# Fourteen tiles fetched by SyncE instead of seven, GpSimd waiting by itself, and 16-bit control tables in a four-layer graph network

## What is computed

```python
h = jnp.maximum(_layernorm(x, axis=-1), 0.0)
x = x + _L0_gnn_ref(...)   # mean of the source rows, times a weight
x = x + _L1_gnn_ref(...)   # sum of h[src] * edge_weight, two products, leaky relu, row norm
x = x + _L2_gnn_ref(...)   # sum of (h W)[src] * network(edge_attr_128), then a small network
x = x + _L3_gnn_ref(...)   # four-head attention: softmax over the edges of each dst
return x
```

## Time and profile before

| | |
|---|---|
| median of three runs | 4121.83 us |
| span of the profiled execution, from its first to its last instruction | 4118.2 us |
| GpSimd busy | 2981.3 us, 72% |
| VectorE, TensorE, ScalarE busy | 2593.0, 2408.9, 1816.6 us |
| gathers by GpSimd (L756) | 3100, mean 945 ns |
| row transfers by SyncE (L805) | 3584 |

### The profile page before, as it was taken

How to read it: one execution, slowest core, us unless ns; L and a number is a source line. 1 busy time by engine, 2 the same in 40 slices (tenths; PEclk the granted TensorE clock), 3 DMA queues, 4 the chain that set the end, 5 groups by cost and what they waited for, 6 DMA issues and landing times. The chain is left out here.

```text
span 4118.2 us, 65293 instructions
## 1 busy us (share of the span) xinstructions
PE 2408.9 (58%) x13340; PEld 2021.0 (49%) x13340; DVE 2593.0 (63%) x7266; ACT 1816.6 (44%) x4202; POOL 2981.3 (72%) x3172
## 2 busy tenths in 40 slices
PE   3666666655566666656544444444566666666667
PEld 2555555554454555546434334443554555454556
DVE  5444444443566666667644444444669999999997
ACT  3444444422243444432211111111457887788886
POOL 4777777776777777777677777777757777777763
PEclk8787777777677787877765666656779999999899
DMA  7444444432344443432333333333466222222221
GB/s 148 125 116 126 116 126 116 126 83 69 94 116 125 116 124 115 126 106 67 100 110 105 110 105 105 110 105 109 115 117 124 58 57 58 57 57 57 57 53 32
DMA packets 242878, 405.96 MB, mean 99 GB/s; under 512 B 68322, under 2 KB 141691, under 8 KB 242492
## 3 DMA queue, kind: packets, MB, share of 16 engines
q0 software_dynamic: 99456, 206.27, 20.8%
q10 hardware_dynamic: 69920, 120.96, 10.4%
q1 hardware_dynamic: 73116, 74.56, 6.2%
HBM read 331.90 MB, written 67.79 MB: 97 GB/s over the span
## 5 line engine op out<-in xcount | busy, mean ns | idle before, releaser
L756 POOL DMA_INDIRECT t_work<-d_T,t_tabG x3100 | 2928.1, 945 | 1038.5 <-issue 848.1
L1657 PE MATMUL ps<-t_work,t_acc 128*128 x2592 | 463.0, 340 | 439.7 <-POOLq L723 396.5
L1657 PEld LDWEIGHTS ps<-t_work,t_acc 128*128 128x128 f32 x2592 | 414.9, 245 | 516.9 <-issue 516.6
L1730 DVE TENSOR_TENSOR t_acc<-t_acc,ps 128x128 f32 (+1 forms) x732 | 210.3, 287 | 513.6 <-PE ps L594 209.5
L1832 ACT COPY ps<-t_acc 128x512 f32 x244 | 140.6, 588 | 779.1 <-POOLq L723 777.1
L1719 DVE TENSOR_TENSOR t_hT<-t_work,ps 128x512 f32<-128x512 f32 x244 | 167.2, 685 | 503.0 <-ACT ps L1832 502.9
L1657 PE MATMUL ps<-t_hT,t_acc 128*128 128x128 f32 x1296 | 264.0, 388 | 272.2 <-DVE t_acc L1730 263.4
L1657 PEld LDWEIGHTS ps<-t_hT,t_acc 128*128 128x128 f32 x1296 | 249.1, 295 | 288.9 <-DVE t_hT L1719 285.0
L1657 PE MATMUL ps<-t_work 128*128 x1312 | 239.9, 347 | 249.7 <-POOLq L723 220.2
L627 ACT ACTIVATE t_acc<-ps,t_bcol 128x1024 f32<-128x1024 f32 x98 | 109.1, 1113 | 612.4 <-DVE ps L640 590.5
L2145 PE MATMUL ps<-t_work,t_hT 128*128 x1960 | 316.8, 310 | 100.2 <-DVE t_acc L2155 81.9
(11 more groups left out here) (205 smaller groups left out, 4478.6 us busy)
## 6 DMA issues: line engine op xcount, KB each, us to landing
d_edge_net<-t_acc ACTq DMA_DIRECT2D x98, 512.0 KB
t_acc<-d_edge_net SPq DMA_DIRECT2D x98, 512.0 KB, 4.2
t_work<-d_T,t_tabG POOLq DMA_INDIRECT x3100
t_acc<-in_edge_attrT ACTq DMA_DIRECT2D x96, 512.0 KB, 4.2
t_acc<-d_T SPq DMA_DIRECT2D x1792, 0.5 KB
t_acc<-d_T SPq DMA_DIRECT2D x896, 0.5 KB
t_work<-d_T SPq DMA_DIRECT2D x896, 0.5 KB
t_acc<-d_T ACTq DMA_DIRECT2D x12, 790.1 KB, 17.0
```

Source lines behind the costliest of these rows:

```text
L756: pool.indirect_dma_start(out=work[:, at:at + width], out_offset=None, in_=table, in_offset=bass.IndirectOffsetOnAxis(ap=idx[:, g * QUAD + ...
L1657: last = pe.matmul(sums(layer, s, width), masks[s % MASKS][:, k, :], rows_k, start=(k == 0), stop=(k == QUAD - 1))
L1730: dve.tensor_tensor(out=o, in0=o, in1=sums(layer, s, width), op=ALU.add).then_inc(e_acc[layer], 1)
```

## The change

SyncE fetches fourteen tiles per layer, ten rows per group; GpSimd leaves out fourteen. The addresses for these rows are loaded 32 at a time, from lists that begin at a multiple of four numbers. The semaphores `e_free` go: GpSimd waits for the sums itself in all layers, against numbers of which it loads 32 at a time; SyncE still waits for each group's sums, ahead of its own work. The tables `ctl`, `closing`, `closing2`, `closingB`, `winB`, `slotB` and `needB` hold 16-bit numbers; in layer 3 TensorE and VectorE read them for two quads at once (needs for eight), in layer 2 ScalarE reads a pair of steps at once. The tables are made in 32 bits beside the others and copied.

```diff
-SIDE, SIDE_PER, SIDE_READ = 7, 5, 64
+SIDE, SIDE_PER, SIDE_READ, SIDE_REGS = 14, 10, 64, 32
...
-        ctl = sb("ctl", [1, 4 * (STEPS + LEAD)], I32)
-        closing, closing2 = sb("closing", [1, GROUPS], I32), sb("closing2", [1, GROUPS], I32)
+        ctl = sb("ctl", [1, 4 * (STEPS + LEAD)], U16)
+        closing, closing2 = sb("closing", [1, GROUPS], U16), sb("closing2", [1, GROUPS], U16)
         relB = sb("relB", [P, TABB])
 
-        winB, slotB = sb("winB", [1, TABB], I32), sb("slotB", [1, TABB], I32)
-        needB, closingB = sb("needB", [1, TABB // QUAD], I32), sb("closingB", [1, GROUPS], I32)
+        winB, slotB = sb("winB", [1, TABB], U16), sb("slotB", [1, TABB], U16)
...
-        e_free = [sem(f"e_free{layer}") for layer in range(3)]
...
+        m_end = V.did(dve.tensor_tensor(out=pair_w, in0=closed_w, in1=steps[0:1, 2:GROUPS + 2], op=ALU.add))
+        need(dve, m, m_end, m_q)
+        m = V.did(dve.tensor_scalar(pair_w, pair_w, 1, None, ALU.arith_shift_right))
...
+        V.did(dve.tensor_copy(closingB[:], quad_w))
...
-        ENDS = 14
+        ENDS = 32
...
-                if layer < 3 and g >= NEAR_FROM:
-                    pool.wait_ge(e_free[layer], g - NEAR + 1)
-                elif layer < 3 and g >= RING:
-                    pool.wait_ge(e_free[layer], g - RING + 1)
-                elif g >= RING:
-                    n = g - RING
+                if g >= RING:
+                    n = g - (NEAR if layer < 3 and g >= NEAR_FROM else RING)
+                    if n == 0 and layer == 0:
+                        need(pool, tables)
...
-                pool.wait_ge(e_free[1], LAST_RAW + 1)
+                pool.wait_ge(used, numbers(ENG.Pool, closed_at[0:1, LAST_RAW - 1:LAST_RAW + 1], 2, 1, top_at)[1])
+                pool.sem_inc(s_go, 1)
...
+        row_from = {}
+
         def fetch_rows(layer, table, n):
 
             row = 4 * table.shape[1]
             table_b = table.rearrange("n w -> (n w)").unsqueeze(0).bitcast(U8)
-            for c in range(SIDE_READS):
-                lo, hi = [min(max(SIDE_PER * m - SIDE_READ * c, 0), SIDE_READ) for m in (n, n + 1)]
-                if lo == hi:
-                    continue
-                if lo == 0:
+            for r in range(SIDE_PER * n, min(SIDE_PER * (n + 1), SIDE * P)):
+                c, at = divmod(r, SIDE_READ)
+                if at == 0:
                     sp.wait_ge(s_src[c % 2], 16 * (SIDE_READS // 2 * layer + c // 2 + 1))
-                found = numbers(ENG.SP, side_sources(layer, c)[:, lo:hi], hi - lo, 0, (N - 1) * row)
-                for r, at in zip(range(c * SIDE_READ + lo, c * SIDE_READ + hi), found):
-                    j, p = divmod(r, P)
-                    sp.dma_start(side_rows(layer, j)[p:p + 1, :].bitcast(U8)[:, 0:row], table_b[:, bass.ds(at, row)])\
-                        .then_inc(s_row[layer][j % 4], 16)
-                if hi == SIDE_READ and c + 2 < SIDE_READS:
+                if at % SIDE_REGS == 0:
+                    row_from[layer] = numbers(ENG.SP, side_sources(layer, c)[:, at:at + SIDE_REGS], SIDE_REGS, 0, (N - 1) * row)
+                j, p = divmod(r, P)
+                sp.dma_start(side_rows(layer, j)[p:p + 1, :].bitcast(U8)[:, 0:row],
+                             table_b[:, bass.ds(row_from[layer][at % SIDE_REGS], row)]).then_inc(s_row[layer][j % 4], 16)
+                if at == SIDE_READ - 1 and c + 2 < SIDE_READS:
                     read_sources(layer, c + 2)
...
-                if n % 4 == 0:
-                    ends = numbers(ENG.SP, closed_at[0:1, n:n + 4], 4, 1, top_at)
+                if n % 8 == 0:
+                    ends = numbers(ENG.SP, closed_at[0:1, n:min(n + 8, GROUPS)], min(8, GROUPS - n), 1, top_at)
...
-                if n > (LAST_FREED[layer] if layer < 3 else GROUPS - RING - 1):
+                if n + RING >= GROUPS + (layer == 2):
                     continue
-                if n + RING < GROUPS:
-                    fetch_rows(layer, table, n)
-                sp.wait_ge(used, ends[n % 4])
-                sp.sem_inc(e_free[layer] if layer < 3 else s_paced, 1)
+                fetch_rows(layer, table, n)
+                sp.wait_ge(used, ends[n % 8])
+                sp.sem_inc(s_paced, 1)
                 if n + RING in SIDE_AT:
                     place_rows(layer, table, pitch, SIDE_AT.index(n + RING))
...
-                edge, _, _, slot = control(ENG.Activation, s)
+                if s % 2 == 0:
+                    found[:] = control_pair(ENG.Activation, s // 2)
+                edge, _, _, slot = found[s % 2]
...
+            v = numbers(engine, slotB[0:1, two_quads(n)], 2 * QUAD, 0, (RING * QUAD - 1) * ROW3)
+            return v[:QUAD], v[QUAD:]
...
+            if n % 2 == 0:
+                rows_at[n], rows_at[n + 1] = slots_of(ENG.PE, n)
+            slots = rows_at[n]
...
-            if add in range(QUADSB):
-                sums_at[add] = numbers(ENG.DVE, winB[0:1, steps_of(add)], QUAD, 0, (BB - 1) * ACC3)
+            if add in range(0, QUADSB, 2):
+                v = numbers(ENG.DVE, winB[0:1, two_quads(add)], 2 * QUAD, 0, (BB - 1) * ACC3)
+                sums_at[add], sums_at[add + 1] = v[:QUAD], v[QUAD:]
...
-            if head in range(QUADSB):
-                rows_of[head] = slots_of(ENG.DVE, head)
+            if head in range(0, QUADSB, 2):
+                rows_of[head], rows_of[head + 1] = slots_of(ENG.DVE, head)
...
-            if head in range(QUADSB) and head % 4 == 0:
-                needs[head // 4] = numbers(ENG.DVE, needB[0:1, head:head + 4], 4, 1, TILES)
+            if head in range(0, QUADSB, 8):
+                needs[head // 8] = numbers(ENG.DVE, needB[0:1, head:head + 8], 8, 1, TILES)
```

More of the change, by code:

```diff
@@ L10 @@
 U8 = mybir.dt.uint8
+U16 = mybir.dt.uint16
 ALU = mybir.AluOpType
@@ L44 @@
 SIDE_READS = SIDE * P // SIDE_READ
-assert P % SIDE_READ == 0
+assert P % SIDE_READ == 0 and SIDE_READ % SIDE_REGS == 0 and SIDE_READS % 2 == 0
 assert SIDE_AT[-1] < GROUPS
@@ L425, in build @@
         need(dve, ld_g.mark)
-        V.did(dve.tensor_scalar(closing[:], lastrow, 7, None, ALU.arith_shift_right))
-        m_shift = V.did(dve.tensor_scalar(closingB[:], lastrow, WB.bit_length() - 1, None, ALU.arith_shift_right))
+        group_w, quad_w, pair_w = (take(GROUPS)[0:1, :].bitcast(I32) for _ in range(3))
+        V.did(dve.tensor_scalar(group_w, lastrow, 7, None, ALU.arith_shift_right))
+        V.did(dve.tensor_scalar(quad_w, lastrow, WB.bit_length() - 1, None, ALU.arith_shift_right))
         m = V.did(dve.tensor_scalar(shifted_g, lastg, 7, None, ALU.arith_shift_right))
         need(dve, m, ld_c.mark)
-        V.did(dve.tensor_copy(closed_w, closing[:]))
+        V.did(dve.tensor_copy(closed_w, group_w))
         closed_q = take(GROUPS)[0:1, :]
@@ L433, in build @@
         need(dve, m_q)
-        m_q = V.did(dve.tensor_tensor(out=closingB[:], in0=closingB[:], in1=closed_q, op=ALU.add))
+        m_q = V.did(dve.tensor_tensor(out=quad_w, in0=quad_w, in1=closed_q, op=ALU.add))
         need(dve, m_q)
-        V.did(dve.tensor_scalar(closingB[:], closingB[:], 2, None, ALU.arith_shift_right))
+        m_q = V.did(dve.tensor_scalar(quad_w, quad_w, 2, None, ALU.arith_shift_right))
         m = V.did(dve.tensor_tensor(out=end_g, in0=shifted_g, in1=cst[:, x0:x0 + 2], op=ALU.add))
@@ L455, in build @@
         V.did(dve.tensor_scalar(ctl3[:, LEAD:STEPS + LEAD, 2], win_s[:, 0:STEPS], float(ACC3), None, ALU.mult))
-        m_end = V.did(dve.tensor_tensor(out=closing[:], in0=closed_w, in1=steps[0:1, 1:GROUPS + 1], op=ALU.add))
-        need(dve, m, m_end)
-        m = V.did(dve.tensor_scalar(closing2[:], closing[:], 1, None, ALU.add))
+        V.did(dve.tensor_tensor(out=closing[:], in0=closed_w, in1=steps[0:1, 1:GROUPS + 1], op=ALU.add))
+        m_end = V.did(dve.tensor_tensor(out=pair_w, in0=closed_w, in1=steps[0:1, 2:GROUPS + 2], op=ALU.add))
+        need(dve, m, m_end, m_q)
+        m = V.did(dve.tensor_scalar(pair_w, pair_w, 1, None, ALU.arith_shift_right))
+        V.did(dve.tensor_copy(closingB[:], quad_w))
         need(dve, m)
-        V.did(dve.tensor_scalar(closing2[:], closing2[:], 1, None, ALU.arith_shift_right))
+        V.did(dve.tensor_copy(closing2[:], pair_w))
         V.did(dve.tensor_scalar(ctl3[:, 0:STEPS + 1, 3], slot_s, float(QUAD * ACC3), None, ALU.mult))
@@ L679, in within @@
             return nc.s_assert_within(v, lo, hi, skip_runtime_bounds_check_because="a part of the staircase's row")
[L681 to L685, removed]
         RAW_GROUP = RING // 2
@@ L778, in side_sources @@
         def side_sources(layer, c):
[L780 to L784, removed]
+            held, lo = (acc, -(-NT * ACC3 // 4) * 4) if layer < 3 else (work, -(-(RING * QUAD + 2) * ROW3 // 4) * 4)
+            assert lo + 2 * SIDE_READ <= (XC if layer < 3 else work.shape[1])
+            return held[0:1, lo + c % 2 * SIDE_READ:lo + (c % 2 + 1) * SIDE_READ].bitcast(I32)
+        assert MLP + 11 * GRP + 2 * ACC3 <= BB * ACC3
```

(16 more changed lines are left out.)

4 lines of the change are left out of this document (2 added, 2 removed).

## The result

The changed kernel takes 4505.69 us (4502.24 to 4507.5) against 4121.64 us beside it: 1.093 times as long, interval 1.0915 to 1.0946. Forecast were 4092 us, in a range of 4080 to 4113. It is slower, and lies above the second rival's 4430 us.

A forecast was written before the change was run, and what follows sets the result against it. GpSimd's gather queue was taken to bound the kernel, four times over. Terms -35.0 + 1 + 2 + 1.3 + 1 = -29.7 us on the 4118.2 us span, plus 3.6 us carried over, gave 4092 us; range 4080 to 4113.

The forecast's parts named there:

- the second rival: VectorE's queue in layer 3, also GpSimd: 16-bit values are read one by one, some 4430 us, slower; chance 13%.
- the price of a 16-bit load: Register loads on GpSimd and VectorE: 32 values at 1.1, 2.1 or 7.2 us; eight at 0.34 or 0.59 us.
- the term that the prediction put at nothing for VectorE: VectorE in layer 3: fewer, eight-value 16-bit loads free its queue of 94 or 26 us, idle time there; taken as 0.
- the first two: GpSimd's loads of 32 16-bit numbers: 1.1 us hides, 2.1 us shows now and then; 2 us charged for 18 loads.
- the third price: GpSimd's loads of 32 16-bit numbers at 0.226 us each: 7.2 us, showing by 4 to 6 us.
- Fewer gathers: GpSimd's gather queue: seven more tiles per layer leave it, 28 gathers x 1.25 us = 35.0 us gained, nothing hides them.
- GpSimd's own wait: GpSimd waits for sums without SyncE's relay: gain between 0 and 20 us, taken as 0; 2 us charged for its loads.
- the charges at the ends of layers 1 and 3: Layer 1's end loses the last tile's 1.3 us; in layer 3 VectorE's lag is charged 1 us.
- SyncE's ten rows: SyncE's group grows by 1.2 us, fitting its idle time: nothing in layers 0 to 2, 1 us charged in layer 3.
- Half of it is taken back: VectorE in layer 3 and the node chain in layer 1 become the bound: gain only 11.5 us, 4110 us; chance 14%.

The follow-up runs named there:

- the runs with 0.60, 0.95 and 1.83 us: Layer 3's winB and slotB loads: 32-bit eights (4100.21 us), 16-bit fours with other tables 32-bit (4233.09 us), 16-bit eights in the changed kernel (4505.69 us).
- the first run: The changed kernel with all seven tables back at 32 bits, waited numbers cut to 16 bits in a register operation: 4100.21 us, ratio 0.995.
- the run with fifteen: Changed kernel with 32-bit tables and GpSimd's loads of eight, SyncE fetching fifteen tiles per layer, eleven rows per group: 4112.91 us, ratio 0.9982.
- the fastest version: The kernel before with fourteen tiles from aligned lists, e_free kept, tables at 32 bits and waited numbers cut: 4089.93 us, ratio 0.9927.
- the loads of four: The changed kernel with 32-bit tables, except winB and slotB at 16 bits, read four at a time in every quad: 4233.09 us, ratio 1.0273.

## Why the prediction was wrong

*The step that failed* is the price of a 16-bit load, and with it the term that the prediction put at nothing for VectorE. On GpSimd the text gave three prices, 1.1, 2.1 and 7.2 us, and said "I take the first two"; on VectorE it took 0 for the eight-value loads because at 0.34 or 0.59 us its queue would be freed (by 94 or 26 us, it says; the second is 552 x 0.34 - 277 x 0.59 = 24). Measured are 7.10 and 1.83 us: the third price, which stood in the second rival with 13%. All my rows were of 32 bits, with one load in the earlier trace rows aligned and one not, and I laid the difference to alignment alone. The quick reads had both, the alignment and the 32 bits; the 16-bit reads have only the alignment, and were slow. With no row on them, the cheap and the dear price should have had like weight.

*The rival had the mechanism, and its sum was near, in part by luck.* It put the decision at a load of some 0.7 us; the runs with 0.60, 0.95 and 1.83 us bracket it there for the addresses. But it came to 0.7 by adding a 0.34 us sum to a 0.34 us load, and what covers the load is one instruction of 0.68 us. It hid a third of VectorE's 404 us less 31, a third that no row gave, and charged 250 us; layer 3 grew by 280 us and the addresses cost 288, near the 245 pauses of 1.15 us that were counted (282). GpSimd's 18 loads were put at 5 us each, 90 us; the sums' tables cost 77.8. It left out `ctl` at the ends of layers 1 and 2 and a longer tail, and its layer 3 was some 30 us too low, so 4430 us became 4506.

*Fewer gathers, -35.0 us:* 33.2 us with GpSimd's own wait (seven against fourteen tiles), 30.0 us alone. With the charges at the ends of layers 1 and 3, 2.3 us, the forecast was 32.7: the term held.

*SyncE's ten rows:* 2.1 us for 32 values were forecast, 2.13 measured. By 1.2 us more per group its 320.9 us of waits in layer 2 should have become 320.9 - 188 x 1.2 = 95 us; they were 87.7 in the first run. It fits, and the run with fifteen shows how closely.

*GpSimd's own wait, taken at 0, with 2 us for its loads:* 10 to 12 us together with the longer reads that go with it. The text bounded the direct wait by a gain of 0 to 20 us and left out a loss; which of these parts lost the time was not found.

*Half of it is taken back* did not happen in layer 1, which gave 8.4 of 8.75 us in the fastest version, and did in layer 3, which gave 4.6: VectorE's waits for announced rows there fell from 31.2 to 8.8 us, so it stood near its own bound. The forecast charged 1 us for that.

The forecast's sum, -29.7 us, is within a microsecond of the kernel with fourteen tiles alone (-30.0), but that is another kernel than the one forecast: the whole change without the width gained 21 us (4121.3 - 4100.2). The change was one part that gained 30 us and others that cost 10; the tables' width turned it round.

## What to carry to other kernels

Before a table is narrowed, look for a row of a load of that width: half the bytes were three times the time here. On VectorE in these runs a register load was free only as far as the instruction already started covered it. So take the length of that instruction from the timeline, and reckon the pauses as load minus cover, times the number of loads. And where one part of a change has a price that no row shows, work out its dear end before counting on the sure gain: here it came to over ten times the 30 us that the fourteen tiles gave.

## What the runs showed of the hardware

- A register load of 16-bit numbers took 0.945 us for 4, 1.83 for 8 and 7.10 for 32, though the reads of 8 and 32 begin at multiples of sixteen bytes; 32-bit numbers read from such multiples took 0.34, 0.60 and 2.03 us (the first run). The 16-bit pace of 0.22 us a number is that of the 32-bit load of 14 that begins off such a multiple (3.16 us).
- VectorE had about 0.7 us of work beside a load where the instruction under way took 0.68 us, and some 0.2 us where it took 0.34. GpSimd lost 5.5 us to a load of 7.1: it went on with two gathers, and the next one began 0.8 us behind the load's end.
- TensorE's granted clock in the mean of layer 3 was 0.90 before, 0.92 with all tables at 32 bits, 0.81 with the loads of four and 0.70 in the changed kernel: it was lower the longer VectorE, for which TensorE waits, stood idle. That the pauses lowered it is read from this order and not tested.
